# Quantized grouped attention, cross product and dense layer in one program: Q's third block taken from exact codes, and what moves with it

## What is computed

```python
q = h @ dequant(q_codes, q_scales)      # 32 heads of 128; one scale per 128 rows and column
k = h @ dequant(k_codes, k_scales)      # 8 heads, each serves 4 Q heads; v likewise
q, k = rope(q), rope(k)
attn = softmax(q @ k.T * 128**-0.5 + causal)
x = x + (attn @ v) @ dequant(o_codes, o_scales)
x = x + fake_quant(layernorm(x)) @ fake_quant(ctx)      # 8-bit rounding of both sides
x = x + layernorm(x) @ binarized(weight).T
```

## Time and profile before

| what | value |
|---|---|
| median of 3 runs | 1063.87 us (1063.73 to 1065.14) |
| the profiled execution, its own time | 1065.44 us |
| its span in the profile | 1063.6 us |
| granted clock of TensorE, mean | 0.996 |
| TensorE, VectorE, ScalarE, GpSimd busy | 96%, 86%, 73%, 74% of the span |
| slots 4 to 7 | 217.91 to 263.75 us |
| slots 8 to 39 (loop, context) | 263.75 to 636.70 us |
| slots 40 to 61 (dense weight) | 636.70 to 888.87 us |

### The profile page before, as it was taken

The page is one execution under the profiler, slowest core; times in us unless marked ns, Lnnn a source line. Parts: engine busy times, 40 slices in busy tenths (PEclk is TensorE's granted clock), DMA queues, the critical chain, the costliest instruction groups (busy, mean ns, idle before and its releaser), DMA issues.

```text
span 1063.6 us, 18927 instructions
## 1 busy us (share of the span) xinstructions
PE 1017.3 (96%) x5286; PEld 500.3 (47%) x5296; DVE 918.9 (86%) x1689; ACT 776.9 (73%) x1677; POOL 790.0 (74%) x817
## 2 busy tenths in 40 slices
PE   5999998899999999999999999999999998989998
PEld 3444343445545455544545455455455454444443
DVE  7989997699888788878878889999999998878873
ACT  5547756788888789888888888888888886453320
POOL 4678887899888778877877889999999998332100
PEclk9999999999999999999999999999999999999999
DMA  9784302776776676666667666777767756513443
GB/s 340 251 193 128 106 26 49 146 153 153 152 170 145 150 156 157 143 149 161 150 139 163 160 138 146 159 155 151 151 159 156 154 133 129 118 81 71 102 98 77
DMA packets 309813, 152.08 MB, mean 143 GB/s; under 512 B 257728, under 2 KB 274240, under 8 KB 309728
## 3 DMA queue, kind: packets, MB, share of 16 engines
q1 hardware_dynamic: 301952, 137.76, 56.8%
q10 hardware_dynamic: 7776, 13.37, 4.3%
HBM read 85.26 MB, written 4.19 MB: 84 GB/s over the span
## 4 chain that ended last, share of the span: by engine, by line
PE 79%; DVE 7%; ACT 5%; issue 4%; POOL 3%; DMA 1%; ACTq 1%; SPq 0%; DVEq 0%; POOLq 0%
PE proj_ps L961 9%; PE out_ps L961 9%; PE side_ps L941 9%; PE side_ps L749 7%; PE side_ps L750 7%; PE side_ps L751 7%; PE side_ps L837 5%; PE proj_ps L1116 5%; PE score_ps L924 3%; PE score_ps L926 3%; PE score_ps L925 3%; PE proj_ps L1121 2%; PE score_ps L1087 2%; PE out_ps L772 1%; PE score_ps L772 1%
## 5 line engine op out<-in xcount | busy, mean ns | idle before, releaser
L1659 POOL TENSOR_SCALAR prob<-prob,row_inv 128x512 f32<-128x512 f32 (+3 forms) x256 | 194.7, 771 | 92.5 <-DVE row_inv L2211 89.6
L1666 POOL TENSOR_TENSOR w_b<-prob,w_b 128x896 f16<-128x896 f32 (+2 forms) x192 | 185.8, 994 | 6.7 <-ACT w_b L1339 6.6
L1312 ACT ACTIVATE prob<-score_ps,neg_max 128x512 f32<-128x512 f32 (+3 forms) x256 | 132.8, 524 | 38.4 <-DVE neg_max L2113 37.1
L2137 DVE SCALAR_TENSOR_TENSOR x_acc<-out_ps,o_now,x_acc 128x1024 f32<-128x1024 f32 x120 | 152.9, 1274 | 1.3 <-PE out_ps L961 1.3
L2137 DVE SCALAR_TENSOR_TENSOR x_acc<-proj_ps,o_now,x_acc 128x1024 f32<-128x1024 f32 x120 | 153.0, 1275 | 0.0
L749 PE MATMUL side_ps<-hT,w_a 128*128 128x512 f16 x384 | 146.0, 380 | 0.1
L750 PE MATMUL side_ps<-hT,w_a 128*128 128x512 f16 x384 | 146.0, 380 | 0.0
L751 PE MATMUL side_ps<-hT,w_a 128*128 128x512 f16 x384 | 145.9, 380 | 0.0
L2113 DVE CUSTOM_DVE_ANT_0 score_ps<-score_ps,mask_b 128x512 f32<-128x512 f32 (+3 forms) x256 | 122.1, 501 | 18.6 <-PE score_ps L926 18.6
L961 PE MATMUL proj_ps<-work,w_b 128*128 128x512 f16 x496 | 127.6, 380 | 3.1 <-issue 1.6
L961 PE MATMUL out_ps<-work,w_b 128*128 128x512 f16 x496 | 127.3, 379 | 0.9 <-DVE x_acc L2137 0.8
(11 more groups left out here) (277 smaller groups left out, 2227.0 us busy)
## 6 DMA issues: line engine op xcount, KB each, us to landing
stage_c<-in_codes_dram SPq DMA_DIRECT2D x72, 256.0 KB, 2.8
stage_o<-in_codes_dram SPq DMA_DIRECT2D x64, 256.0 KB, 3.3
stage_s<-in_scales_dram SPq DMA_DIRECT2D x34, 256.0 KB, 3.7
ctx_raw<-in_ctx_dram ACTq DMA_DIRECT2D x32, 256.0 KB, 3.3
work<-w_b SPq DMA_TRANSPOSE x261, 3.0
x_acc<-in_x_dram SPq DMA_DIRECT2D x8, 512.0 KB, 8.3
k_sb<-in_codes_dram SPq DMA_DIRECT2D x16, 256.0 KB, 7.0
v_sb<-in_scales_dram SPq DMA_DIRECT2D x16, 256.0 KB, 7.1
```

The costliest lines, as they stand in the source:

```text
L1312: ins = act.activation(prob[:, SCORE_AT[qb]:SCORE_AT[qb] + w], score_ps[:, score_bank(i, u), off:off + w], ACT.Exp, bias=neg_max[:, c:c + ...
L1659: return pool.tensor_scalar(prob[:, at:at + w], prob[:, at:at + w], row_inv[:, col:col + 1], P_UP, ALU.mult, ALU.mult)
L1666: ins = pool.tensor_tensor(prob16[:, 1, to:to + w], prob[:, at:at + w], prob16[:, 0, to:to + w], ALU.subtract)
L2137: ins = dve.scalar_tensor_tensor(y, u, s, y, ALU.mult, ALU.add)
```

## The change

Q's first three blocks (instead of two) are taken from exact codes. For each of 60 slots TensorE has a third `q_exact` (two matmuls) and `q_part` covers blocks 3 to 7 (15 matmuls instead of 18). ScalarE has a third `q_base`, which stands behind `o_cut` and ahead of `exps` of unit 1. On TensorE `q_exact(2)` stands behind O unit 0 and ahead of the third score unit, and O unit 1 moves from behind `q_part` to ahead of it. The subtraction of 128 from the context codes moves from ScalarE (behind `q_hi`) to VectorE (behind the second `reciprocal`). Every other `q_cut`, `piece_scale` and `piece_lo` covers 128 instead of 256 columns, and its exact codes 384 instead of 256. The ratios take 10 small steps instead of 7, and `q_ratio` lies in the last 64 columns of `ctx_raw`. The steps of K's last tile move to the end of the slots, and the wait for the tile from slot 3 to slot 7.

```diff
-N_EXACT = 2
+N_EXACT = 3
+RATIO_STEPS = 3 * N_EXACT + 1
@@ TensorE, q_exact and q_part
-                    pe.wait_ge(q_based, 2 * (p - FIRST_PIECES) + 1)
+                    pe.wait_ge(q_based, N_EXACT * (p - FIRST_PIECES) + e)
...
-                        pe.wait_ge(q_based, 2 * (p - FIRST_PIECES) + 2)
+                        pe.wait_ge(q_based, N_EXACT * (p - FIRST_PIECES) + N_EXACT)
@@ TensorE, scores
-                    if known(p) and p == O_LAG:
+                    if known(p) and p == SLOTS - 1:
                         pe.wait_ge(k_ready, K_TILES)
@@ TensorE, slot
-                if has_o and not (known(p) and p == O_LAG):
+                if known(p) and p == O_LAG:
+                    o_unit(p, i, 0)
+                elif has_o:
                     o_unit(p - 1, prev[1], 3)
                 scores(p, i, g, 1)
                 if has_ahead and parts:
                     q_exact(*ahead, 1)
                 if v_at:
                     v_blocks(v_at[2], v_at[3])
                 if has_o:
-                    o_unit(p, i, 0)
+                    o_unit(p, i, int(known(p) and p == O_LAG))
+                if has_ahead and parts:
+                    q_exact(*ahead, 2)
...
                 scores(p, i, g, 2)
...
+                if has_o and not (known(p) and p == O_LAG):
+                    o_unit(p, i, 1)
                 if has_ahead:
                     q_part(*ahead, range(N_EXACT if parts else 3, KB))
                 if has_o:
-                    o_unit(p, i, 1)
                     o_unit(p, i, 2)
@@ ScalarE, slot
                 if has_ahead and by_parts(p + Q_AHEAD):
                     q_base(*next_q, 0)
+                exps(p, i, 0)
+                if has_ahead and by_parts(p + Q_AHEAD):
+                    q_base(*next_q, 1)
+                o_cut(p, i)
+                if has_ahead and by_parts(p + Q_AHEAD):
+                    q_base(*next_q, 2)
+                if has_next and not by_parts(p + 1):
+                    q_hi(p + 1)
+                exps(p, i, 1)
+                if known(p) and wf_late(p) is not None:
+                    wf_upper(wf_late(p))
+                exps(p, i, 2)
                 if known(p) and p == 1:
                     late_swaps()
                 if known(p) and p == 2:
                     late_upper()
-                exps(p, i, 0)
-                if has_ahead and by_parts(p + Q_AHEAD):
-                    q_base(*next_q, 1)
-                if has_next and not by_parts(p + 1):
-                    q_hi(p + 1)
-                o_cut(p, i)
-                exps(p, i, 1)
...
-                if with_ctx:
-                    act.wait_ge(ctx_scaled, q + 1)
-                    act.activation(dst, ctx_codes, ACT.Copy, bias=-Q_MID).then_inc(ctx_free, 1)
@@ VectorE, slot
                 if has_next and by_parts(p + 1):
                     q_sum(p + 1)
-                if known(p) and p < 3:
-                    (late_join, late_sum, late_lower)[p]()
+                if known(p) and p == 0:
+                    late_join()
...
                 dve.reciprocal(row_inv[:, 3:4], row_sum[:, 3:4]).then_inc(inv_ready[1], 1)
+                if with_ctx:
+                    q, dst = ctx_half(g, i)
+                    dve.wait_ge(ctx_scaled, q + 1)
+                    dve.tensor_scalar(dst, ctx_codes, Q_MID, None, ALU.subtract).then_inc(ctx_free, 1)
...
                     wf_difference(wf_early(p))
+                if known(p) and 0 < p < 3:
+                    (late_sum, late_lower)[p - 1]()
                 if has_o:
                     o_add(p, i, 1)
                     o_add(p, i, 2)
```

More of the change, by code:

```diff
@@ L108 @@
 RATIO_FROM = 4
-RATIO_STEPS = 7
 CB = D // P
@@ L252, in build @@
         scal = sb("scal", [P, 11], F32)
-        q_ratio = sb("q_ratio", [P, NH], F32)
         ones_b = sb("ones_b", [P, P], BF16)
@@ L257, in build @@
         ctx_codes = ctx_raw[:, 0:S // 4].bitcast(U8)
+        q_ratio = ctx_raw[:, S - (N_EXACT - 1) * NH:S].rearrange("p (h e) -> p h e", e=N_EXACT - 1)
         sums = sb("sums", [P, 8], F32)
@@ L1288, in q_base @@
                 p = g * SLOTS + i
-                act.wait_ge(q_exact_done, 2 * (p - FIRST_PIECES) + (e + 1))
+                act.wait_ge(q_exact_done, N_EXACT * (p - FIRST_PIECES) + (e + 1))
                 if known(p) and p < Q_LEAD * B:
@@ L1391, in slot @@
                 if with_ctx:
-                    q, dst = ctx_half(g, i)
+                    q, _ = ctx_half(g, i)
                     tile = ctx_rows[bass.ds((g - 1) * 4 + i // 2, 1), :, (i % 2) * S:(i % 2 + 1) * S]
@@ L1402, in slot @@
                     late_upper()
-                exps(p, i, 0)
-                if has_ahead and by_parts(p + Q_AHEAD):
-                    q_base(*next_q, 1)
-                if has_next and not by_parts(p + 1):
-                    q_hi(p + 1)
-                o_cut(p, i)
-                exps(p, i, 1)
-                if known(p) and wf_late(p) is not None:
-                    wf_upper(wf_late(p))
-                exps(p, i, 2)
                 if with_ctx:
@@ L2042, in ratio_step @@
                 rows = q_scale_rows.rearrange("p (h k) -> p h k", k=KB)
-                by = q_ratio[:, :]
+                by, of = q_ratio[:, :, :], rows[:, :, 1:N_EXACT]
                 per = stats.rearrange("p c h n -> p (c h n)")[:, 0:NH]
@@ L2048, in ratio_step @@
                     dve.wait_ge(scale_rows_landed, 32)
+                e = (k - 3) // 3
                 if k == 0:
-                    ins = dve.tensor_tensor(by, rows[:, :, 1], rows[:, :, 1], ALU.mult)
+                    ins = dve.tensor_tensor(by, of, of, ALU.mult)
                 elif k == 1:
@@ L2053, in ratio_step @@
                 elif k == 2:
-                    ins = dve.tensor_tensor(by, by, rows[:, :, 1], ALU.add)
-                elif k == 3:
-                    ins = dve.reciprocal(per, by)
-                elif k == 4:
-                    ins = dve.tensor_tensor(per, rows[:, :, 0], per, ALU.mult)
-                else:
-                    row, up = ((per, 1.0), (by, Q_UP))[k - 5]
-                    c = CB + k - 5
+                    ins = dve.tensor_tensor(by, by, of, ALU.add)
+                elif k < RATIO_STEPS - 1 and k % 3 == 0:
+                    ins = dve.reciprocal(per, by[:, :, e])
+                elif k < RATIO_STEPS - 1 and k % 3 == 1:
+                    ins = dve.tensor_tensor(per, by[:, :, e - 1] if e else rows[:, :, 0], per, ALU.mult)
+                else:
+                    row, up = (per, 1.0) if k < RATIO_STEPS - 1 else (by[:, :, N_EXACT - 2], Q_UP)
+                    c = CB + e
                     dve.tensor_scalar(o_table[:, 0:NH - Q_LEAD, c], row[:, Q_LEAD:NH], up, None, ALU.mult)
@@ L2155, in ao_rest, with slot @@
                     .then_inc(ao_ready, 1)
-            def slot(g, i):
+            def slot(g, i, with_ctx):
                 p = g * SLOTS + i
@@ L2235, in body @@
                 for i in range(SLOTS):
-                    slot(g, i)
+                    slot(g, i, with_ctx)
             def x1_part():
```

## The result

The changed kernel takes **1091.49 us** (median of 4 runs, 1091.36 to 1092.61). The kernel before, run beside it, takes 1064.51 (4 runs, 1063.73 to 1067.41). The ratio is 1.025 (95% interval 1.023 to 1.027): slower by 27 us, where 24.1 was forecast from the loops. The profiled execution has a span of 1090.8 us.

A forecast was written before the change was run, and what follows sets the result against it. TensorE paced slots at 11.46 us; after the change, handover loops through ScalarE and VectorE would bound them. 9.0 + 15.1 + 2.0 - 2.5 + 0.5 = +24.1 us on 1063.87 gave 1088 us, range 1075 to 1100.

The forecast's parts named there:

- The loop through ScalarE, 11.74: Context slots: handovers from one `q_copy` to the next sum to 11.74 us, above TensorE's 11.46, and so bound the slot.
- The loop through VectorE, 12.04: Dense-weight slots: VectorE's list plus handovers sum to 12.04 us, 0.58 over the pace; 26 slots, 15.1 us more.
- The term 32 x 0.28 = 9.0 us for slots 8 to 39: The 32 context slots each take 0.28 us more than TensorE's 11.46: 9.0 us more.
- the stops at the branches: Three TensorE stops of 1.96 us at the loop's branches back, left unchanged since ScalarE comes as late as before.
- Ratios, +2.0: K projection, taken as bound by VectorE: three more ratio steps and double width for three cost +2.0 us (0 to 2.5).
- Slot 3, -2.5: Slots 1 to 3: less TensorE waiting for `q_base(0)`, K's last tile no longer delaying: -2.5 us (0 to -3.5).
- Tail, +0.5: End of kernel: slot 61's exponentials come about 0.5 us later in the slot, +0.5 us (0 to 1.3).
- Context codes on VectorE, 0: Moving the subtraction from ScalarE to VectorE costs 0, hidden by 1.42 us of VectorE waiting behind the new place.
- The rival of the clock: TensorE's new gaps in each slot drop the clock in a tenth of slots: 29 us more, 1117 us; chance 0.02.
- The rival of the dissolving overlap on VectorE: `wf_difference` no longer overlaps GpSimd, 0.70 instead of 1.38 us; all slots about 11.75, total 1081 us; chance 0.15.

The follow-up runs named there:

- ao_first: Changed kernel with ScalarE running `ao_part` ahead of the second `prob_split` (last slot keeps its order): 1072.65 us.
- base1_first: Changed kernel with ScalarE running `q_base(1)` ahead of the exponentials of unit 0 instead of behind them: 1073.97 us.
- o1_late: Changed kernel with TensorE running O unit 1 behind `q_part` again, as in the kernel before: 1095.03 us.
- two_exact: Changed kernel with two exact blocks of Q instead of three (no third exact pair or `q_base`, seven ratio steps), all else kept: 1088.86 us.
- x2_late: Changed kernel with TensorE running the third exact pair of Q behind the third score unit instead of ahead of it: 1086.24 us.
- x2_copy: As x2_late, and VectorE copies `o_now` behind the maxima of unit 0 instead of ahead of them: 1075.97 us.
- m0_first: Changed kernel with VectorE taking the maxima of unit 0 ahead of `ao_rest` and the copy of `o_now`: 1058.02 us.
- m0_x2: Changed kernel with the order changes of m0_first and x2_late together: 1067.92 us.

## Why the prediction was right, and where not

- **The loop through ScalarE, 11.74**: right. 11.74 and 11.81 in turn were measured, the links within 0.05 of the rows that they were taken from, and the run that shortens one link moved the context slots as the sum says (`ao_first` 11.31 and 11.53). `base1_first` (11.57) and `o1_late` (11.91) came out as I had expected too, but there TensorE's own list with short waits for `q_base` and the exponentials is the bound, and they say nothing of the sum of 11.74.
- **The loop through VectorE, 12.04**: right in half of the slots, those of 12.08, where VectorE goes from the third maxima to the end of the first in 9.58 us without a pause (787.79 to 797.37). In the slots of 11.95 it stands 0.36 us for `q_cut` and 0.30 for `ao_part`, so their path runs through ScalarE, and `ao_first` shortened them alone. That the mean of 12.02 fits to 0.02 is in part luck. Slots 4 to 7 were 12.27 and then 11.95 to 12.08.
- **The term 32 x 0.28 = 9.0 us for slots 8 to 39 was too small**: 13.2. The step that failed is that I left the copy of `o_now` at its mean length, 0.06 of the way to the maxima. Four slots paid 1.2 us each for it, 4.9 together; 0.8 came from the slots of 11.81, and the stops at the branches, which I had left as they were, took 39.8 us together instead of 40.6 and gave 1.6 back. (The three stops before were 1.96, 1.93 and 1.76 us, not 1.96 each.) In `two_exact` and `x2_late` the same copy is the largest term of all, so the forecast of the total was right also because GpSimd ran in another phase here.
- **Ratios, +2.0: wrong.** The first score matmul started at 166.59, 0.7 earlier. The eight kernels with three exact blocks differ only in the slots and have it at 166.54 to 167.25, so the 0.7 is no clear gain, but a loss of 2 us is out. VectorE did get three more steps in the K projection, but they were not on the path there. A busy 58.02 of 60 us was taken for a bound. The ratio step of the earlier trace rows, 1.26 us for 128x29, was probably itself a held instruction: it started at 128.50 and ended within 0.05 us of a GpSimd `tensor_tensor` (128.06, 1.65 us long). `two_exact`, with seven steps again, had its first score matmul at 168.02, no earlier.
- **Slot 3, -2.5**: -2.1 for slots 2 and 3. TensorE's wait fell from 2.27 to 0.87 and the granted clock stayed at 1.00 where it was 0.83:

```profile
206.82 0.61 PE L837 MATMUL side_ps<-hT,w_a 128*128 128x512 f16 x2 [0.87 <-ACT side_ps L1299]
...
205.00:210.00 5.00, 3.61 (x21) 1.60 (x20) 1.61 (x7) 4.82 (x12) 4.95 (x6) 1.00 0.79 129
```

- **Tail, +0.5**: 1.75, of which 0.8 lies in slots 62 and 63 and 1.0 behind the last slot; I have not followed it.
- **Context codes on VectorE, 0**: right. The subtraction takes 0.77 us and no wait in the list above leads to it. No run took this part of the change out by itself.
- **The rival of the clock**: some 60 new stops of 0.3 to 1.0 us, one in each slot, and four of 1.5 us left the granted clock at 1.00 in both windows. What the Trainium skill says of idle times between groups (TensorE: Matmul & The Clock Gate, section A second HAM failure mode: psum-queue depth-cycling) did not happen with these.
- **The rival of the dissolving overlap on VectorE**: it did not come; `wf_difference` took 1.28 and 1.37 us in turn. But the contention with GpSimd that it was about was the right place to look, only in the other direction: overlap came about where there had been none. I had weighed only the instructions with two inputs in SBUF; the one that decided slots has a single input of 11 columns. The GPSIMD Engine Reference of the Trainium skill (section Key points) names, beside the two-input instructions, those in a 2-port performance mode, and I passed over these.

The sum by stretches: up to slot 1 -0.3, slots 2 and 3 -2.1, 4 to 7 +2.4, 8 to 39 +13.2, 40 to 61 +12.2, behind them +1.8, together +27.2 against the profiled span of before.

## What to carry to other kernels

A full TensorE does not tell how near the next bound is. Follow each handover once around a slot, add the links, and do so for every loop that the change touches; then a change is a number on a link, and the cheapest cure (here one line of order on VectorE, worth 33 us) can be read from the same sum. Do not put a short instruction at its mean length into such a chain: look at its longest case and at what runs on GpSimd beside it, and put it where nobody waits.

## What the runs showed of the chip

**A tiny copy on VectorE can last as long as the GpSimd instruction beside it.** 128x10 or 128x11 words from SBUF to SBUF took 0.16 us by themselves, 1.26 to 1.31 beside a `tensor_tensor` of 1.26, 0.77 beside one of 0.72, and 0.66 when started 0.64 us into one of 1.27; each time both ended within 0.05 us of each other. The maxima, which read PSUM, kept their 0.69 us beside a GpSimd `tensor_tensor` of 1.26 or 1.27 (375.72 above, beside one that started at 375.73, and 416.57 in x2_copy, beside the one of 416.54). A second case is `piece_lo` (L1876 here, 128x128), which has two inputs in SBUF. In `m0_first` it stands beside GpSimd's L1683; two of its slots show both outcomes. Started 0.01 us behind it it took 1.29 us, started 0.06 us ahead of it 0.29, and then GpSimd took 1.25 instead of 1.15:

```profile
364.39 1.15 POOL L1683 TENSOR_TENSOR q_sb<-rot,q_sb 128x512 f16<-128x512 f32 x1
364.40 1.29 DVE L1876 SCALAR_TENSOR_TENSOR w_a<-stage_s,w_a 128x128 f16<-128x128 f32 x1 [0.42 <-ACT w_a L1202]
...
432.46 0.29 DVE L1876 SCALAR_TENSOR_TENSOR w_a<-stage_s,w_a 128x128 f16<-128x128 f32 x1 [0.35 <-ACT w_a L1202]
432.52 1.25 POOL L1683 TENSOR_TENSOR q_sb<-rot,q_sb 128x512 f16<-128x512 f32 x1
```

The Trainium skill has the rule (SBUF — State Buffer, section SBUF: two separate sides): VectorE and GpSimd have a pair of ports in common, which one of them locks for its whole instruction while the other stands; on VectorE's side it concerns two inputs in SBUF and the 2-port mode, which a copy of float32 inside SBUF takes. The traces agree, with 1.26, 0.77 and 0.66 us for the rest of GpSimd's instruction, and 0.69 for the maxima that were let through. GpSimd's instruction went first where it had the lead (422.25 against 422.29) and also where the copy's recorded start was 0.02 us earlier (784.15 against 784.17). With 0.05 or 0.06 us of lead VectorE's did (432.46 against 432.52; the copy at 616.62 in the changed kernel, against 616.67, took 0.17). No run measured the effect by itself, outside this kernel. Read before the change, the rule and the 0.59-us mean of the same copy in the dense-weight slots of the kernel before, against 0.19 in the context slots, would have said that this copy can take 1.3 us in the chain. These are its groups of the kernel before, slots 8 to 39 and then 41 to 61:

```profile
L2123 DVE COPY o_now<-work 128x10 f32 x16 | 3.0, 187 | 0.0
...
L2123 DVE COPY o_now<-work 128x10 f32<-128x10 f32 x10 | 5.9, 591 | 0.0
```

**A stop of TensorE of about 2 us costs the clock in one place and not in another.** In `m0_first` two stops of equal length ended differently: the one before 356.93, 1.95 us, was followed by 4.5 us at a granted clock of 0.62 (mostly the 1.2 GHz level), the one before 451.16, also 1.95 us, by 1.00. After 3.40 us in `m0_x2` it was 0.61. The ten traces of this case have 30 such stops at a branch. Seven were followed by 4.5 us at 0.62 or 0.63: the three of 3.40 to 3.44 us in `m0_x2`, 2.12 and 2.06 in `ao_first`, 1.99 in `o1_late` and the 1.95 here. The other 23, of 1.59 to 2.03 us, were followed by 1.00. The two stops of 1.95 us stand in slots of 15.05 and 13.43 us, so the drop cost about 1.6 us.
